# A graph network's nearest-row search: squared norms by four row-group matmuls side by side, distance tiles in two rounds

## The reference, cut to what matters

```python
x = layernorm(x + adj @ (scale * (adj @ (x @ w0))) + bias)        # products 0 and 1
x = layernorm(x + relu(rownorm(adj') @ x @ W.T + b))              # product 2
z = leaky_relu(lap(adj) @ x @ W1 + b1)                            # product 3
d2 = |z_i|^2 + |z_j|^2 - 2 z_i.z_j                                # the search
S = exp(-sqrt(d2) / 2), kept for the 4 nearest j of every i
x = layernorm(x + lap(S + adj) @ x @ W2 + b2)                     # product 4 + gathered rows
x = layernorm(x + relu([x, adj @ x] @ W.T + b))                   # product 5
```

## Time and profile before

| | |
|---|---|
| median of 3 runs | 1494.22 us (1489.24 to 1497.74) |
| span of the profiled execution, its own time | 1494.6 us |
| PE busy | 1424.5 us, 95% |
| DVE busy | 835.5 us, 56% |
| ACT busy | 467.3 us, 31% |
| POOL busy | 258.8 us, 17% |
| HBM traffic | 271 GB/s over the span |
| chain that ended last | PE 73%, DVE 12%, DMA 12% |

### The profile page before, as it was taken

One profiled execution on the slowest core, in us unless ns is written; L12 is line 12 of the kernel. 1 busy time (PEld: TensorE's weight loads), 2 busy tenths in 40 slices (PEclk: granted clock), 3 DMA queues, 4 the chain that ended last, 5 costly groups with the idle time before them and its releaser, 6 DMA issues.

```text
span 1494.6 us, 20312 instructions
## 1 busy us (share of the span) xinstructions
PE 1424.5 (95%) x7300; PEld 761.3 (51%) x7300; DVE 835.5 (56%) x1310; ACT 467.3 (31%) x979; POOL 258.8 (17%) x381
## 2 busy tenths in 40 slices
PE   6999999999998799999999987999999799999997
PEld 4776666666443344444444443444444344444454
DVE  6877776665234323333222289999999255564044
ACT  4776665564000000000000056666666200000011
POOL 2111111011000000000000001211111477774000
PEclk9999999999999999999999999999999889999999
DMA  9999998998998969779778420014334889999862
GB/s 307 403 384 378 361 334 304 332 321 292 392 389 303 393 235 354 307 307 336 293 286 310 176 71 1 15 43 127 114 113 127 288 295 368 372 386 394 344 250 74
DMA packets 115934, 406.41 MB, mean 272 GB/s; under 512 B 10416, under 2 KB 31504, under 8 KB 94096
## 3 DMA queue, kind: packets, MB, share of 16 engines
q1 hardware_dynamic: 77264, 319.58, 57.5%
q0 software_dynamic: 20144, 75.50, 13.2%
q10 hardware_dynamic: 18448, 10.28, 2.3%
HBM read 340.82 MB, written 64.49 MB: 271 GB/s over the span
## 4 chain that ended last, share of the span: by engine, by line
PE 73%; DVE 12%; DMA 12%; ACT 1%; issue 1%; ACTq 0%; DVEq 0%; SPq 0%; POOLq 0%
PE acc L1098 11%; PE acc L1100 11%; PE acc L1099 11%; PE pt L1162 5%; DVE wz_sb L984 4%; DMA region<-at_scratch 4%; DMA region<-in_adj 3%; DVE hT L983 3%; DMA at_scratch<-region 3%; PE pt L1099 3%; PE pt L1100 3%; PE pt L1098 3%; PE pt L1238 2%; PE pt L1241 2%; PE pt L1240 2%; PE pt L1239 2%
## 5 line engine op out<-in xcount | busy, mean ns | idle before, releaser
L1098 PE MATMUL acc<-region,yop 128*128 128x512 f16 x693 | 265.2, 383 | 19.0 <-DMA region<-at_scratch 18.8
L1100 PE MATMUL acc<-region,yop 128*128 128x512 f16 x693 | 264.9, 382 | 0.0
L1099 PE MATMUL acc<-region,yop 128*128 128x512 f16 x693 | 264.8, 382 | 0.0
L1162 PE MATMUL pt<-ident,region 128*128 128x128 f32 x1024 | 242.9, 277 | 20.7 <-DMA region<-in_adj 15.6
L646 ACT ACTIVATE region<-pt 128x512 f32<-128x512 f32 x256 | 150.9, 597 | 107.1 <-PE pt L1241 84.6
L1162 PEld LDWEIGHTS pt<-ident,region 128*128 128x128 f32 x1024 | 145.7, 143 | 61.8 <-DMA region<-in_adj 10.8
L932 DVE SCALAR_TENSOR_TENSOR region<-pt,region 128x512 f16<-128x512 f32 x200 | 135.3, 687 | 71.6 <-ACT region L602 71.2
L602 ACT ACTIVATE region<-pt 128x512 f16<-128x512 f32 x200 | 117.5, 596 | 104.3 <-PE pt L1162 84.4
L983 DVE MAX8 hT<-region 128x8 f32<-128x4096 f32 x32 | 141.3, 4415 | 4.4 <-ACT region L646 4.4
L1098 PEld LDWEIGHTS acc<-region,yop 128*128 128x128 f16 x693 | 68.2, 98 | 101.4 <-DMA region<-at_scratch 13.4
L571 ACT ACTIVATE std<-mv,eps_ln 128x4 f32<-128x4 f32 x32 | 9.5, 297 | 333.2 <-DVE mv L767 333.2
(11 more groups left out here) (225 smaller groups left out, 2212.9 us busy)
## 6 DMA issues: line engine op xcount, KB each, us to landing
region<-at_scratch SPq DMA_DIRECT2D x169, 1280.0 KB, 7.8
region<-in_adj SPq DMA_DIRECT2D x64, 1024.0 KB, 9.6
at_scratch<-region POOLq DMA_DIRECT2D x40, 768.0 KB, 7.4
at_scratch<-region POOLq DMA_DIRECT2D x40, 512.0 KB, 7.4
region<-at_scratch SPq DMA_DIRECT2D x77, 256.0 KB, 3.8
x_scratch<-xout ACTq DMA_DIRECT2D x24, 256.0 KB, 12.1
xin<-at_scratch SPq DMA_DIRECT2D x12, 256.0 KB, 2.9
xout<-at_scratch SPq DMA_DIRECT2D x12, 256.0 KB, 4.4
```

Source lines behind the costliest of these rows:

```text
L1098: nc.tensor.matmul(into, y[:, 0, kt, :], high, start=(kt == first_tile), stop=False)
L1099: nc.tensor.matmul(into, y[:, 0, kt, :], low, start=False, stop=False)
L1100: return nc.tensor.matmul(into, y[:, 1, kt, :], high, start=False, stop=(kt == last_tile))
L1162: ins = nc.tensor.transpose(pt[kt % 4][:, t * P:(t + 1) * P], nat[u % 4][:, t, (kt % TPC) * P:(kt % TPC + 1) * P], ident[:, :])
```

## The change

The squared norms of four banks are added by four matmuls that use 3 rows each of four groups of 32 rows of the array. `sqT` therefore holds the three parts of chunk j in the partitions from 32 (j % 4) on, `ones3` is one everywhere, and the transposes and copies of the squares are over all 128 partitions. A row of tiles goes through four banks in two rounds: `first_banks` makes the 3 x 4 matmuls of banks 0 to 3 and then the four of the squares, `second_banks` the same for banks 4 to 7, with the copies of the second round in the order 7, 4, 5, 6. Row 0 still uses three banks. Each row from 8 to 31 has a wide unit, half of it between the two rounds and half behind the second; 24 units are in the search and 8 behind it. `pe_project_x2` moves from row 4g+6 to row 4g+8. A memset of `gath_all` at the start goes and one of `xT` ahead of the third pass comes.

```diff
-NEAR_BANKS = 3
+NEAR_BANKS = 4
+FIRST_BANKS = 3
+GROUP = 32
+COPY_ORDER = [0, 1, 2, 3, 7, 4, 5, 6]
-WIDE_AT = {8: 0, 9: 1, 11: 2, 12: 7, 14: 3, **{i: i - 8 for i in range(16, 32)}}
+WIDE_AT = {i: i - 8 for i in range(8, 32)}
-WIDE_REST = [4, 5, 6, 24, 25, 26, 27, 28, 29, 30, 31]
+WIDE_REST = [24, 25, 26, 27, 28, 29, 30, 31]
...
-            pool.memset(ones3[:, :], 0.0).then_inc(ident_made, 1)
+            pool.memset(ones3[:, :], 1.0).then_inc(ident_made, 1)
-            pool.memset(gath_all[:, :, :, :], 0.0).then_inc(consts, 1)
-            pool.memset(ones3[0:3, :], 1.0).then_inc(consts, 1)
...
-                        step(nc.vector.tensor_copy(sq_parts[par][:, :, k], sq_rest[:, 0:TPC]))
+                        step(nc.vector.tensor_copy(sq_parts[par][:, :, :, k],
+                                                   sq_rest[:, 0:TPC].unsqueeze(2).to_broadcast([P, TPC, NEAR_BANKS])))
...
             step(nc.vector.tensor_copy(ident16, ident[:, :]))
+            step(nc.vector.memset(sq_spread, 0.0))
...
+            def squares(i, j):
+                cols = slice(j * CHUNK, (j + 1) * CHUNK)
+                group = slice(j % NEAR_BANKS * GROUP, j % NEAR_BANKS * GROUP + 3)
+                nc.tensor.matmul(near_bank(i, j)[:, :], ones3[group, :], sqT[group, cols], start=False, stop=True
+                                 ).then_inc(near_full, 1)
...
+            def first_banks(i):
+                g, step_of = divmod(i - TPC - 2, TPC)
+                for j in range(NEAR_BANKS):
+                    if i == 1 and j < FIRST_BANKS:
+                        pe.wait_ge(near_copied, max(copies(0, k) for k in range(NCH) if k % FIRST_BANKS == j))
+                    if i > 1:
+                        pe.wait_ge(near_copied, copies(i - 1, j + NEAR_BANKS))
+                    if j == NEAR_BANKS - 1 and g >= 0 and step_of == 0:
+                        pe.wait_ge(xT_ready, nth(XTS, 4, g))
+                    if j == NEAR_BANKS - 1 and g >= 0 and step_of == 3:
+                        pe.wait_ge(yw_ready, g + 1)
+                    closeness(i, j)
+                for j in range(NEAR_BANKS):
+                    squares(i, j)
+
+            def second_banks(i):
+                for j in range(NEAR_BANKS, NCH):
+                    pe.wait_ge(near_copied, copies(i, j - NEAR_BANKS))
+                    closeness(i, j)
+                for j in COPY_ORDER[NEAR_BANKS:]:
+                    squares(i, j)
...
-            for i in range(KT):
-                if i > 0:
-                    closeness(i, range(NCH))
+            for i in range(1, KT):
+                first_banks(i)
+                if i in WIDE_AT:
+                    wide_products(WIDE_AT[i], range(WIDE // 2))
+                second_banks(i)
+                if i in WIDE_AT:
+                    wide_products(WIDE_AT[i], range(WIDE // 2, WIDE))
                 g, step_of = divmod(i - TPC - 1, TPC)
                 if g >= 0 and step_of == 0:
+                    pe.wait_ge(near_copied, copies(i, NCH - 1))
                     pe_turn(pe, 4, g)
-                if g >= 0 and step_of == 1:
+                if g >= 0 and step_of == 3:
+                    pe.wait_ge(near_copied, copies(i, NCH - 1))
                     pe_project_x2(pe, g)
-                if i in WIDE_AT:
-                    wide_products(WIDE_AT[i])
```

More of the change, by code:

```diff
@@ L188, in sq_bank, with near_bank, copies @@
         def sq_bank(par):
-            return pt[3][:, :].bitcast(BF16)[0:3, par * CHUNK:(par + 1) * CHUNK]
+            return pt[3][:, :].bitcast(BF16)[:, par * CHUNK:(par + 1) * CHUNK]
+        def near_bank(i, j):
+            return pt[j % (NEAR_BANKS if i > 0 else FIRST_BANKS)]
+        def copies(i, j):
+            return i * NCH + (COPY_ORDER.index(j) if i > 0 else j) + 1
         wide = [acc[0][:, :], acc[1][:, :], pnat[:, :, :].rearrange("p t f -> p (t f)"), pxT[:, :]]
@@ L643, in copy_near @@
                 for j in columns:
-                    n = i * NCH + j
-                    act.wait_ge(near_full, n + 1)
-                    nc.scalar.activation(near[i % 2][:, j * CHUNK:(j + 1) * CHUNK], pt[n % NEAR_BANKS][:, :],
+                    act.wait_ge(near_full, copies(i, j))
+                    nc.scalar.activation(near[i % 2][:, j * CHUNK:(j + 1) * CHUNK], near_bank(i, j)[:, :],
                                          ACT.Copy).then_inc(near_copied, 1)
@@ L700, in _ @@
                         act.wait_ge(near_used, i - 1)
-                    copy_near(i, range(NCH))
+                    copy_near(i, COPY_ORDER)
                 g, step_of = divmod(i - TPC - 1, TPC)
@@ L1082, in pe_squares @@
             for t in range(TPC):
-                last = nc.tensor.transpose(sq_bank(par)[:, t * P:(t + 1) * P], sq_parts[par][:, t, :], ident16)
+                last = nc.tensor.transpose(sq_bank(par)[:, t * P:(t + 1) * P],
+                                           sq_parts[par][:, t, :, :].rearrange("p q r -> p (q r)"), ident16)
             last.then_inc(sqT_full, 1)
@@ L1227, in _, with closeness @@
             product_pass(3, 2)
[L1230 removed]
+            def closeness(i, j):
                 zh, zl = (zT[:, h, i * P:(i + 1) * P] for h in range(2))
[L1232 to L1241 removed]
+                cols = slice(j * CHUNK, (j + 1) * CHUNK)
+                into = near_bank(i, j)[:, :]
+                nc.tensor.matmul(into, zh, zT[:, 0, cols], start=True, stop=False)
+                nc.tensor.matmul(into, zh, zT[:, 1, cols], start=False, stop=False)
+                nc.tensor.matmul(into, zl, zT[:, 0, cols], start=False, stop=False)
@@ new lines, in squares, with first_row @@
+            def squares(i, j):
+                cols = slice(j * CHUNK, (j + 1) * CHUNK)
+                group = slice(j % NEAR_BANKS * GROUP, j % NEAR_BANKS * GROUP + 3)
+                nc.tensor.matmul(near_bank(i, j)[:, :], ones3[group, :], sqT[group, cols], start=False, stop=True
+                                 ).then_inc(near_full, 1)
+            def first_row(columns):
+                for j in columns:
+                    if j >= FIRST_BANKS:
+                        pe.wait_ge(near_copied, copies(0, j - FIRST_BANKS))
+                    closeness(0, j)
+                    squares(0, j)
@@ L1249, in _ @@
             pe_turn(pe, 3, NCH - 1)
-            closeness(0, range(3, 5))
+            first_row(range(3, 5))
             pe_squares(pe, NCH - 1, 1)
-            closeness(0, range(5, NCH - 1))
+            first_row(range(5, NCH - 1))
             pe.wait_ge(sqT_ready, NCH)
@@ L1255, in _, with wide_products @@
             pe.wait_ge(late_loaded, 16 * LATE_PARAMS)
-            closeness(0, range(NCH - 1, NCH))
-            def wide_products(kt):
+            first_row(range(NCH - 1, NCH))
+            def wide_products(kt, columns=range(WIDE)):
                 pe.wait_ge(yop_ready, nth(YOP, "y", kt // TPC))
-                for c in range(WIDE):
+                for c in columns:
                     if kt < KEPT:
@@ L1286, in _ @@
                 if n == 0:
+                    pe.wait_ge(near_copied, copies(KT - 1, NCH - 1))
+                    pe_project_x2(pe, NCH - 2)
+                if n == 1:
                     pe_turn(pe, 4, NCH - 1)
-                if n == 1:
+                if n == 2:
                     pe_project_x2(pe, NCH - 1)
```

23 lines of the change are left out of this document (7 added, 16 removed).

## The result

The changed kernel takes 1512.42 us (median of 5 runs, 1504.57 to 1512.93), the kernel before, run beside it, 1497.41 (5 runs, 1489.24 to 1499.65). The ratio is 1.0101 with a 95% interval of [1.0078, 1.0124]: 1% slower. The prediction was 1496.5 with a range of 1480 to 1512. Its range was missed by 0.4 us, its forecast by 16.

A forecast was written before the change was run, and what follows sets the result against it. The prediction took the DVE, then TensorE, then transfers to bound the kernel. It summed 1494.6 us + 1.65 for later gathers + 0.3 for the lower clock to 1496.5 us, with a range of 1480 to 1512.

The forecast's parts named there:

- Part 1: Squares in the search: grouped matmuls replace 32 per four rows, which take 36.1 us instead of 39.31 without a new wait.
- G: Cost of one group of four squares matmuls with both changes of array shape: 0.46 us, bounds 0.22 and 1.06.
- Rival 3: A group of squares costs a drain, G = 0.61, adding 6.3 to E: 1503 us, slower; chance 0.12.
- rival 4: The four squares streams don't run side by side, G = 1.06, adding 29 to E: 1525 us; chance 0.13.
- Part 2: Search: TensorE waits 2.7 us for POOL's operand in every fourth row from 8; E = 1174.1, 5.8 later than before.
- Part 3: Behind the search, 11 units become 8; the gathers start at E + 21.4 instead of E + 25.5, 1.65 us later than before.
- E: The end of the last index search, which ends the search: 1168.33 before, predicted 1174.1.
- The end of the wide part: Last wide unit behind the search: E + 26, from 6.6 MB of transfers taking 22 us, instead of E + 41.
- That the end follows the gathers: Behind the search, the second projection waits for the DVE's residual behind the gathers, so TensorE would stand idle there.
- "+0.3" for the clock: Behind the search, TensorE leaves its stop at the lower clock for about 5 us, eating the slack: +0.3 us.
- rival 1: In the search, the wait does not bite or the groups are nearly free: E = 1159, total 1481 us; chance 0.20.
- rival 2: Behind the search, the gathers' data come early enough and TensorE keeps its lead of 9 us: 1485 us; chance 0.08.

The follow-up runs named there:

- experiment 3: The change's two parts apart: 24 wide units put into the kernel before (1.0067), and the changed kernel with the old 21 units (1.0093).
- experiment 4: Changed kernel with bank 4's products repeated three times in rows 8, 12, ..., 28 to fill TensorE's wait for POOL: 1505.08 us, ratio 1.0057.
- 24 units, old squares: Kernel before with 24 wide units in rows 8 to 31 and 8 behind the search, squares and banks as before: ratio 1.0067.
- experiment 1: Changed kernel with the whole wide unit behind the second round of banks in rows 8, 12, 16, 20, 24 and 28: ratio 1.0001.
- experiment 6: The four residual loads of x2 issued by ACT's queue instead of POOL's: ratio 1.0063 in the changed kernel, 1.0020 in the kernel before.
- new squares and 21 units: Changed kernel with the units where they stood before, 21 in the search and 11 behind it: ratio 1.0093.
- full squares: Changed kernel with the squares over the full array again, four matmuls one behind the other in place of each group: ratio 1.0147.

## Why the prediction was wrong, step by step

**What bounds the kernel: right.** DVE, TensorE and transfers in turn; and, as part 2 had it, the operand's chain of ACT and POOL in rows 4g+8, where TensorE waits for it even with fewer units to do (2.67 and 2.74 us, experiment 3).

**Part 1: right.** G is 0.42 instead of 0.46, the streams are side by side, the changes cost 0.2. Rival 3 (0.61) and rival 4 (1.06) are out.

**Part 2 failed in the step that priced the wait.** "It waits 2.7 us in rows 8, 12, 16, 20, 24 and 28": the wait is 2.67, in just these rows. But the text priced it by its length alone, "four rows take 36.1 + 2.7 = 38.8", and kept TensorE at its 0.2155 step behind it. In four of the six rows the clock fell behind the wait and eight steps took 0.43: 1.7 us each, of which row 8 passed 0.7 on. That is 0.7 + 3 x 1.7 = 5.8 us, the difference between the 308.54 measured and the 302.7 predicted, and experiment 4 gives it back: 302.85. That the rest fits to 0.2 us is in part luck: in experiment 4 row 12 comes 0.8 later than predicted, and the four periods behind it are shorter by 0.7 together. The prediction knew of the lower clock behind a stop and booked it for one in the rest, not for those that it had itself put into the search.

**Part 3 failed in two terms, E + 21.4 against E + 28.4.** "I take 7 of 11.1" was a guess between two bounds, with the reason that SP's loads would be ahead of the residual loads. It measured 11.92, and 11.1 to 13.5 in every kernel where POOL issues the four loads, whatever was in SP's queue: +4.9. It ended each time with the landing of the third load, 0.38 us ahead of the fourth issue. And "the chain to the last y, which the change doesn't touch" was wrong: the change puts unit 24 first in the rest, where units 4, 5 and 6 with a long finished operand had stood, and the turn of group 7 now waits behind it and unit 25, where it had stood behind the first unit alone: +2.0. It takes both the order and the long wait of unit 24: with the same unit first in the old order it waits 2.95 us instead of 5.58, and the last store stays at E + 9.7 (24 units, old squares). The second term was to be had from the diff; for the first, had the wait, and the trace of before the landing with which it ended.

The end of the wide part, E + 26, came at E + 33: unit 24 began with a wait of 5.58 us, and two of 3.27 and 3.03 followed. The time didn't hang on it.

**That the end follows the gathers: right for the changed kernel**, and so was the idle time that it announced (7.62 us). The size behind it was short: "+0.3" for the clock, where the stretch from the gathers on took 1.2 more than before. Over all runs it takes 279.4 to 280.5 from the second projection to the end where TensorE came to it with a wait of at most 1.75 us, and 281.6 to 283.9 where it had waited 4 us or more.

**The sum.** -1.0 (start of the search) + 5.8 + 7.0 + 0.9 = 12.7, the distance from 1496.5 to the span of 1509.3 up to rounding. The other 3.1 to the median of 1512.42 are two things. The time of an execution is longer than its span, here 1510.91 against 1509.3, a term that the prediction put at nothing ("which is its time here"); and the other 1.5 are the spread of the executions.

**Rivals.** 1 and 2 did not come: the wait bit, and the rest was not freed. The result lies at the "slower" that had 0.26, reached by none of the rivals: the forecast's own mechanism with three terms that all went one way. The condition of rival 1, no wait, was met by experiment 1 (a search of 292.89), and even then the time was that of before, not the 1481 of the rival. Its search of 287.6 (to an E of 1159) was missed by 5.3, as four rows took 36.7 and not 36.1, and rows 8 to 12 took 38.2; and the end follows the gathers and the residual rows, and the gathers stayed at E + 29.5. In rival 4 the 29 us are 8 x 6 groups of 0.6; by the count of rival 3, 7 x 6, they would be 25. It changes no verdict.

**Left open.** Why the clock fell behind the wait in rows 8, 12, 20 and 24 and not in 16 and 28 of the same execution, nor behind the 2.95 us that unit 24 waits with the old squares; why POOL's fourth load goes only when the third has landed; and whether the 7.74 us that the first gather waits for the last store of y (experiment 6) can be cut. None was tried.

## What to carry to other kernels

A stall on TensorE is priced twice, by its length and by the steps at the lower clock behind it: here 2.7 us of waiting cost 4.4 in two rows out of three, and to fill the wait with work thrown away paid. Where a change puts a wait ahead of half of a row's work, look for the work that used to stand between the operand's producer and its first use, and put the first use behind it (here one condition, worth 15 us of search). And where the end follows a chain of loads, look at what the change does to that chain: from E to the end the changed kernel lost 4.1 us against before, and experiment 1 lost 6.1, more than the 4.1 by which its search was shorter. With POOL's fourth load and the late turn out of the way the gain of the search showed (0.9966), and earlier residual loads gave another 8.5 us behind E (0.9890).

## What the hardware showed that I had not expected

- Behind waits of TensorE of the same 2.67 us the granted clock fell to the lower level in four rows and stayed in two. The first step at double length came 0.3 to 1.1 us after the work had begun again, and it lasted some 3.4 us. In another profile the very first step behind such a wait was slow (0.40 us, row 16 with new squares and 21 units). Behind five waits of 1.60 us (full squares) it never fell; behind one of 1.79 us in row 8 it fell in three of five profiles.
- POOL's fourth load of 512 KB was held for 11.09 to 13.50 us in all eight profiles where POOL issues these loads, and in each it went 0.38 us behind the landing of the third. On ACT's queue, issued in one go, the last two of the four took 12.3 to 17.5 us together (four profiles); with two of them issued 13 us ahead of the others none took over 0.8.
- Four matmuls of 3 rows in four row groups took 0.39 to 0.40 us as a block; a single one of the same shape, in row 0, took 384 to 385 ns.
